# A two-layer graph kernel on one core: its SBUF tensors declared in another order, behind a pad of 384 bytes

## What is computed

```
h = relu(layernorm(x))
H = (adj != 0);  Dn = 1 / (H @ adj[0]);  Be = 1 / H.sum(axis=1)
layer 0:  conv(v, W, b) = Dn * (H @ (Be * (H^T @ (v @ W^T)))) + b
          y = conv(layer_norm(relu(conv(h, W1, b1))) , W2, b2) + h
x = x + y
h = relu(layernorm(x))
layer 1:  Xw = h @ Wv + bv;  e = leaky_relu(sj + si + ab)
          T = A * exp(e), rows normalised
          H = h @ Wk[0] + T h @ Wk[1] + T T h @ Wk[2] + biases
x = x + relu(H)
```

## The kernel before

| stage | matmuls a step | columns | moving, its offset | stationary, its offset |
|---|---|---|---|---|
| U | 16 | 512 | `inct` 0 | `part_b` 32 |
| V, two parts | 24 + 24 | 256 | `p_hi`, `p_lo` 32 | `a_hi`, `a_lo` 64 |
| Z | 24 | 512 | `w1_hi`, `w1_lo` 0 | `part_a` 32 |
| transposes of `xl`, `si`, `r_sb` | 28 | 128 | `ident` 64 | `xl`, `r_sb` 32, `si` 96 |
| Y2 | 24 | 258 | `wk_hi` 0, `wk_lo` 32, rows + 8 | `xt_hi`, `xt_lo` 32 |
| Y10 | 24 | 512 | `wk_hi`, `wk_lo` 8 to 48 | `xt_hi`, `xt_lo` 32 |
| Y | 48 | 256 | `w2_hi`, `w2_lo` 0 | `part_a`, `part_b` 32 |
| M | 32 | 258 and 256 | `h_hi` 0 to 24, `h_lo` 32 | `inc` 0 |
| G | 32 | 256 | `part_a` 32 | `inc` 0 |
| P | 48 | 258 and 256 | `y2_hi` 32 to 56, `y2_lo` 64 | `a_hi`, `a_lo` 64 |
| O | 32 | 256 | `g_hi`, `g_lo` 32 (views of `xt_hi`, `xt_lo`) | `inct` 0 |

## Time and profile before

### The profile page before, as it was taken

How to read it: one execution, slowest core, us unless ns; L and a number is a source line. 1 busy time by engine, 2 the same in 40 slices (tenths; PEclk the granted TensorE clock), 3 DMA queues, 4 the chain that set the end, 5 groups by cost and what they waited for, 6 DMA issues and landing times.

```text
span 838.3 us, 16609 instructions
## 1 busy us (share of the span) xinstructions
PE 811.9 (97%) x5766; PEld 757.6 (90%) x5766; DVE 643.8 (77%) x1726; ACT 475.9 (57%) x1001; POOL 431.5 (51%) x596
## 2 busy tenths in 40 slices
PE   6888999999999999999999999999999999999997
PEld 5686999999999998999999899998989999899986
DVE  4769777878878787887778887777887877777565
ACT  3334738365573836657384674738457482754644
POOL 3657264573736547363654736365482736632242
PEclk9989999999999999999999999999999999999999
DMA  8131302204041220403122040312204031110001
GB/s 276 64 101 42 124 13 77 89 26 139 0 126 36 75 88 8 155 0 125 38 75 88 0 163 0 124 39 75 88 0 163 0 110 54 52 51 1 26 19 34
DMA packets 39807, 57.82 MB, mean 69 GB/s; under 512 B 2528, under 2 KB 20960, under 8 KB 39776
## 3 DMA queue, kind: packets, MB, share of 16 engines
q1 hardware_dynamic: 39776, 57.42, 20.7%
HBM read 49.03 MB, written 8.39 MB: 68 GB/s over the span
## 4 chain that ended last, share of the span: by engine, by line
PE 92%; DVE 4%; ACT 2%; issue 1%; DMA 1%; POOL 1%; SPq 0%; DVEq 0%
PE ps L699 86%; PE ps L886 3%; PE ps L831 1%; PE ps L875 1%; DMA r_sb<-in_adj 1%; DVE inct L1375 0%; POOL p_lo L421 0%; DVE inc L1038 0%; DVE st_x L1017 0%; ACT e_sb L575 0%; DVE r_sb L1171 0%; ACT h_f L510 0%; DVE x L1414 0%; ACT e_sb L581 0%; DVE st_r L1177 0%
## 5 line engine op out<-in xcount | busy, mean ns | idle before, releaser
L407 POOL TENSOR_TENSOR y<-y,bk_row 128x256 f32<-128x256 f32 x64 | 56.3, 909 | 207.9 <-DVE a_lo L1247 207.9
L699 PE MATMUL ps<-w_hi,part_a 128*128 128x256 f32 (+1 forms) x512 | 158.0, 344 | 4.9 <-DVE part_b L1234 2.7
L699 PE MATMUL ps<-w_lo,part_a 128*128 128x256 f32 (+1 forms) x384 | 124.3, 324 | 0.0
L699 PEld LDWEIGHTS ps<-w_hi,part_a 128*128 128x128 f32 x512 | 98.2, 192 | 17.6 <-issue 3.0
L699 PE MATMUL ps<-wk_hi,xt_hi 128*128 128x258 f32 (+1 forms) x256 | 89.4, 349 | 3.3 <-DVE xt_lo L1069 1.8
L699 PE MATMUL ps<-wk_hi,xt_lo 128*128 128x258 f32 (+1 forms) x256 | 86.7, 339 | 0.0
L699 PE MATMUL ps<-wk_lo,xt_hi 128*128 128x258 f32 (+1 forms) x256 | 86.6, 338 | 0.0
L699 PEld LDWEIGHTS ps<-w_lo,part_a 128*128 128x128 f32 x384 | 74.4, 194 | 5.8
L1241 DVE TENSOR_TENSOR e_sb<-e_sb,adjt_sb 128x512 f32<-128x512 f32 x64 | 44.2, 691 | 44.8 <-ACT e_sb L581 44.8
L411 POOL TENSOR_TENSOR xt_lo<-xl,xt_hi 128x256 fp32r<-128x256 f32 x60 | 57.0, 978 | 39.2 <-ACT xt_hi L655 39.1
L699 PE MATMUL ps<-w_hi,part_b 128*128 128x256 f32 x256 | 73.5, 287 | 0.0
(11 more groups left out here) (144 smaller groups left out, 2524.8 us busy)
## 6 DMA issues: line engine op xcount, KB each, us to landing
adjt_sb<-in_adj_t SPq DMA_DIRECT2D x16, 1024.0 KB, 5.3
adj_sb<-in_adj SPq DMA_DIRECT2D x31, 512.0 KB, 3.6
xin<-in_x SPq DMA_DIRECT2D x15, 512.0 KB, 4.5
out_dram<-x SPq DMA_DIRECT2D x15, 512.0 KB, 3.3
w_row<-in_adj SPq DMA_DIRECT2D x16, 256.0 KB, 3.5
e_sb<-in_w_t SPq DMA_DIRECT2D x2, 512.0 KB, 9.8
y<-in_wk SPq DMA_DIRECT2D x3, 256.0 KB, 4.5
xin<-in_x SPq DMA_DIRECT2D x4, 128.0 KB, 2.3
```

The costliest lines, as they stand in the source:

```text
L407: pool.tensor_tensor(y10[:, t, D:], y10[:, t, D:], bk_row[:, :], ALU.add).then_inc(po_y0, 1)
L699: return pe.matmul(dst, stationary, moving, start=first, stop=last, skip_group_check=True)
```

## The change

The tensors are declared in another order, and a new tensor of 384 bytes, which nothing reads or writes, stands ahead of them. Nothing else in the text of the program differs. Four groups follow one another: the pad; all tensors with rows of a round size, those of the weights with them; the four with rows of 258 or 770 elements; the narrow ones.

```
--- before
+++ after
@@
+        ahead_of_matrices = sb("ahead_of_matrices", [96], F32)
         xin = sb("xin", [TI, D], F32)
...
         h_f = sb("h_f", [TI, D], F32)
-        h_hi = sb("h_hi", [TI, D2], F32R)
         h_lo = sb("h_lo", [TI, D], F32R)
...
-        y2_hi = sb("y2_hi", [TI, D2], F32R)
         y2_lo = sb("y2_lo", [TI, D], F32R)
...
         a_lo = sb("a_lo", [TI, C], F32R)
-
+        w1_hi = sb("w1_hi", [TD, HID], F32R)
+        w1_lo = sb("w1_lo", [TD, HID], F32R)
+        w2_hi = sb("w2_hi", [TH, D], F32R)
+        w2_lo = sb("w2_lo", [TH, D], F32R)
+        ident = sb("ident", [P], F32)
...
+        h_hi = sb("h_hi", [TI, D2], F32R)
+        y2_hi = sb("y2_hi", [TI, D2], F32R)
+        wk_hi = sb("wk_hi", [TD, WX], F32R)
+        wk_lo = sb("wk_lo", [TD, WX], F32R)

         st_x = sb("st_x", [8, 6], F32)
...
```

More of the change, by code:

```diff
@@ L130, in build @@
         xl = sb("xl", [TI, D], F32)
-        g_f = xl
         xt_hi = sb("xt_hi", [TI * D], F32R)
         xt_lo = sb("xt_lo", [TI * D], F32R)
-        g_hi = xt_hi[:, :].rearrange("p (c n) -> p c n", n=D)
-        g_lo = xt_lo[:, :].rearrange("p (c n) -> p c n", n=D)
         p_hi = sb("p_hi", [TI, D], F32R)
         p_lo = sb("p_lo", [TI, D], F32R)
-        y2_hi = sb("y2_hi", [TI, D2], F32R)
         y2_lo = sb("y2_lo", [TI, D], F32R)
@@ L144, in build @@
         a_lo = sb("a_lo", [TI, C], F32R)
+        w1_hi = sb("w1_hi", [TD, HID], F32R)
[3 more added lines that the diff above has]
+        ident = sb("ident", [P], F32)
+        b1_row = sb("b1_row", [HID], F32)
+        b2_row = sb("b2_row", [D], F32)
+        bk_row = sb("bk_row", [D], F32)
+        c0_row = sb("c0_row", [D], F32)
+        h_hi = sb("h_hi", [TI, D2], F32R)
+        y2_hi = sb("y2_hi", [TI, D2], F32R)
+        wk_hi = sb("wk_hi", [TD, WX], F32R)
+        wk_lo = sb("wk_lo", [TD, WX], F32R)
         st_x = sb("st_x", [8, 6], F32)
@@ L170, in build @@
         si = sb("si", [TI], F32)
[L173 to L183, removed]
         gam_c = sb("gam_c", [TH], F32)
@@ L189, in build @@
         c_e = sb("c_e", [1], F32)
+        g_f = xl
+        g_hi = xt_hi[:, :].rearrange("p (c n) -> p c n", n=D)
+        g_lo = xt_lo[:, :].rearrange("p (c n) -> p c n", n=D)
         w1_f = e_sb[:, 0:TD, :]
```

## The result

The kernel after takes 842.71 us in the median of 14 runs (840.06 to 843.9), the one before 839.63 in 14 runs (837.58 to 844.78). The ratio is 1.0028 with a 95% interval of 1.0015 to 1.0041: slower by about 2.3 us by the ratio (the two medians are 3.1 us apart), a quarter of a per cent. That lies inside the range, but on the side opposite to the 834.6 us forecast.

A forecast was written before the change was run, and what follows sets the result against it. TensorE's matmul distances, without waits in the middle, bound the kernel. Four stage terms sum to 5.3 us less: 840.09 to 834.8, set at 834.6 us to match the runs' median; range 827 to 846.

The forecast's parts named there:

- the reading of the address: Stationary operand's offset modulo 128 sets the pace of 256-column matmuls: 0 gives 116.6 ns, 64 gives 118.3, 32 gives 119.8.
- G and O: Stages of 32 matmuls, 256 columns, stationary already at offset 0: stay at 116.6 ns, no change.
- V: Stage of 24 matmuls, 256 columns, stationary at 64: 118.3 to 116.6 ns, 1.3 us less.
- Y: Stage of 48 matmuls, 256 columns, stationary at 32: 119.8 to 116.6 ns, 2.5 us less.
- M: Stage with stationary at 0, half its moving operands of 258 columns, 118.4 ns: no change.
- U and Z: Stages of 16 and 24 matmuls with 512 columns, stationary at 32: no change.
- P: Stage of 48 matmuls, two thirds with 258 columns, stationary at 64: 119.6 to 118.4 ns, 0.9 us less.
- Y2: Stage of 24 matmuls with 258 columns, stationary at 32: 120.0 to 118.4 ns, 0.6 us less.
- The slower rival: Third rival: equal offsets make moving and weight reads disturb each other; 845.1 us, or 851.4 if 512 columns follow; chance 0.22.
- The larger gain: Rival: alignment on 512 bytes removes up to 10 ns per matmul in all stages, 772 us, a fifth 822; chance 0.26.
- no change: Rival: the order of the operands sets the pace, not their place; 839.9 us, chance 0.16.
- The term of the four tensors with long rows: `y2_hi`, `wk_hi`, `wk_lo` and `h_hi`, moving operands only: zero effect, bounds within the 2 ns already counted.

The follow-up runs named there:

- experiment 1: Separate kernel computing nothing of the reference: 68 chains of 32 matmuls at chosen operand offsets; equal offsets took 119.8 to 120.0 ns with 256 columns.
- experiment 7: Kernel after the change with `inc` and `inct` alone moved by 224 bytes: 836.83 us, ratio 0.9963 to the kernel before.
- layout_32: Whole kernel with tensors reordered, aiming at moving minus stationary offset 32 in 256-column stages and 0 in 512-column ones: 831.68 us, ratio 0.9912 to the kernel before.
- experiment 4: Chains-only kernel like that of experiment 1: 89 chains, finer offset differences and patterns of the real stages; 113.3 ns at 192, but 117.8 for the pattern of three.

## Why the prediction was wrong

**What bounds the kernel**: right. In every whole kernel run here the middle is TensorE's alone and it waits for nobody there, so the length of a step tells each layout's cost.

**The step that failed** is the reading of the address: "it orders the stages of 256 columns by their **stationary** operand", with the sentence behind it, that the moving operand doesn't order them. Three values (116.6 at 0, 118.3 at 64, 119.8 at 32) were fitted by one variable, and the difference fits the same three as well: 32 in G and O, 224 in V, 96 in Y. The prediction looked at each operand by itself and never at the two together, though its third rival did. Its offsets modulo 128 hid the pattern besides: by them the difference is 96 in V and in Y, which have different paces, and only modulo 256 do they part. Chains at four equal pairs of offsets (experiment 1) and G with `inc` at 96 (experiment 7) settle it. What the runs showed in its place is the difference of the two offsets. From that one step came all four terms of the sum, and the zeros of G, O and M; those of U and Z came from the sentence on 512 columns:

| term | forecast, us | measured, us | how |
|---|---|---|---|
| V | -1.3 | +1.0 | 2 x 0.03 x 16 |
| Y | -2.5 | -0.2 | 0.01 x 16 |
| P | -0.9 | +0.3 | 0.02 x 16 |
| Y2 | -0.6 | -0.2 | 0.01 x 16 |
| G and O | 0 | +3.4 | 0.21 x 16 |
| M | 0 | +0.6 | 0.04 x 16 |
| U and Z | 0 | -3.4 | 0.21 x 16 |
| Y10 | 0 | +0.5 | 0.03 x 16 |

**The slower rival** had the right mechanism at 256 columns: both streams at one offset are the slow case, and V, M, G and O together lost 5.0 us where its price was 5.2. Its extension was wrong in sign. It gave the stages of 512 columns, if they followed, a loss in proportion, 6.3 us more (845.1 to 851.4), and U and Z won 3.4, which is what left the change at +2.2 and not at +5.2. Nothing in the trace of before had 512 columns at a difference of 0, but for the two matmuls of the earlier trace rows, which were used as evidence against this rival. Their 235 ns are the beginning of a chain: in experiment 1 the chain at 0 and 0 with 512 columns comes down to 226.7 only after such a start (229.1 with it). So that row could not tell, and it took chance away from the case that came nearest. That it came nearest is in part luck: its price of 5.2 was taken from Y's pace, which is by chance close to the pace at a difference of 0 (119.9 at 96, 120.0 at 0).

**"I take it that loading the weights is covered there"** was wrong too: with 512 columns the difference is worth 226.7 to 236.7 ns in the chains, as much as with 256.

**The larger gain** and **no change**: half a truth each. The stages had room, down to 113.3 ns (256 columns) and 226.7 (512), where the rival saw 107, but alignment on 512 bytes is not what gives it. And the order of the operands doesn't explain the changes: it was the same in all seven whole kernels here. It isn't nothing, though: at a difference of 192 the pattern of three took 117.8 ns and the one of blocks 113.3. The term of the four tensors with long rows, put at zero, came out small and not zero: 0.3 us in P, 0.5 in Y10, -0.2 in Y2, in stages where the partner moved too.

**The other zeros** held: the other engines, the ends and the pad (no run tells more of the ends than that their scatter is wider than 2 us). The Trainium skill, TensorE: Matmul & The Clock Gate, "NX overlap", gives N cycles between matmuls back to back; no chain here came there, the shortest distance is 113.3 ns for 256 columns at a granted clock of 1.00, with 107 by that rule. The Trainium skill, SBUF — State Buffer, "Who interferes with whom", gives the weights and the moving operand independent read ports; taken to mean that their addresses don't matter to each other, the runs do not agree (113.3 to 120.2 ns with 256 columns by the difference).

**What would show it** worked as written: "if G and O rise, it is the slower rival", and they did; that U and Z take part was to be seen in their windows, and was.

**What stays open**: why the difference acts, and in opposite ways at 256 and 512 columns. The runs show the dependence and its period of 256 bytes, no mechanism. Open too is what makes a stage at one difference settle at one pace or another: at 192 at 113.4 (G) or 117.8 (O, and the pattern of three), at 32 at 116.6 (O before) or 118.1 (O in `layout_32`). The order of the matmuls, those that ran before, and the absolute place are candidates that no run separates.

## What to carry to other kernels

Where a kernel is one engine's chain, divide each stage's start-to-start time by its count and ask of every reading which other variable fits the same values, above all the relation between two operands that are read at the same time. Aligning all operands alike is no neutral choice: here it makes nearly all meet at a difference of 0, which cost V, M, G and O 5.0 us and gave U and Z 3.4. Before laying out SBUF anew, spend one run on chains of the matmuls in question at chosen offsets: such a run's table led to 0.99 of the time, with the text of the program unchanged but for its declarations. Then read each stage again in the kernel itself, since a chain's pace need not be the stage's.

## What the runs showed of the hardware

- The time from one `float32r` matmul to the next, each with its own weight load, goes with the first byte of the moving operand minus that of the stationary, modulo 256: 113.3 to 120.2 ns with 256 columns in steps of 16 bytes (experiment 4), 226.7 to 234.3 with 512. A difference of 4 bytes is the worst of those tried: 123.3 and 236.7 (experiment 1).
- One difference can have two paces: 113.3 and 117.8 ns at 192 with 256 columns, 228.7 and 233.3 at 64 with 512.
- The shortest are 113.3 / 256 and 226.7 / 512, both 0.443 ns a column, which at a granted clock of 1.00 is 17/16 of a cycle of 2.4 GHz.
- Fewer columns don't go below 111.7 ns (128 and 192 columns, each with a weight load of its own); 320 take 146.7 and 384 take 173.4 at a difference of 0, 176.7 at 32.
- A chain's first matmuls are slower behind a short one: over 32 of them it adds 1 to 3 ns to the mean.
